# Four buffers of gathered expert rows instead of three

## The reference

```python
x = x + tanh(g_xattn) * attn(layernorm(x), ctx)   # attn: gelu(xn @ ctx.T) @ ctx, per batch
x = x + tanh(g_ffn) * moe(layernorm(x), gate_w, w1, w2, w3)

# moe: 8 experts, 256 hidden numbers each; every row goes to its two best experts
scores = softmax(xf @ gate_w); top_scores, top_idx = top_k(scores, 2)
xs = top_score * xf
y += (silu(xs @ w1[e]) * (xs @ w3[e])) @ w2[e]     # for both experts e of the row
```

## Time and profile before

| what | us |
|---|---|
| median of 3 runs | 688.33 |
| lowest and highest | 687.57, 690.29 |
| the profiled execution, its own time | 688.32 |
| its span (first to last instruction) | 686.6 |
| PE busy | 636.1 (93%) |
| POOL busy | 395.6 (58%) |
| ACT busy | 460.6 (67%) |
| DVE busy | 416.9 (61%) |
| mean granted TensorE clock, share of full | 0.991 |

### The profile page before, as it was taken

How to read it: one execution, slowest core, us unless ns; L and a number is a source line. 1 busy time by engine, 2 the same in 40 slices (tenths; PEclk the granted TensorE clock), 3 DMA queues, 4 the chain that set the end, 5 groups by cost and what they waited for, 6 DMA issues and landing times.

```text
span 686.6 us, 15832 instructions
## 1 busy us (share of the span) xinstructions
PE 636.1 (93%) x4638; PEld 442.9 (65%) x4639; DVE 416.9 (61%) x1287; ACT 460.6 (67%) x771; POOL 395.6 (58%) x459
## 2 busy tenths in 40 slices
PE   2789999999999999999998999999999999999990
PEld 1677788788887888878885555455554554555550
DVE  3368788898889888898886644543333333333330
ACT  5899999899998999999974444444443444434440
POOL 4332347765666656776566777875555555565551
PEclk9999999999999999999999999999999999999996
DMA  7455558646686567666424565766666656666653
GB/s 216 128 171 157 160 150 200 182 143 181 163 171 195 160 154 189 174 170 179 119 83 120 93 132 93 121 102 120 111 108 121 117 100 122 111 108 118 118 102 55
DMA packets 51380, 94.77 MB, mean 138 GB/s; under 512 B 17024, under 2 KB 25344, under 8 KB 51312
## 3 DMA queue, kind: packets, MB, share of 16 engines
q1 hardware_dynamic: 34096, 60.02, 32.9%
q0 software_dynamic: 16400, 33.89, 27.6%
q10 hardware_dynamic: 816, 0.02, 0.1%
HBM read 61.89 MB, written 32.01 MB: 137 GB/s over the span
## 4 chain that ended last, share of the span: by engine, by line
DMA 26%; PE 11%; issue 5%; DVE 3%; POOL 3%; ACT 1%; POOLq 1%; SPq 0%; DVEq 0%; ACTq 0%
DMA out_rows<-ctx_raw,meta 23%; PE bank L1368 5%; DMA ctx_raw<-xf_rows,meta 3%; PE bank L1377 3%; POOL out_rows L537 2%; PE bank L1323 1%; POOLq L533 1%; PE bank L1357 1%; ACT ctx_raw L766 1%; DMA meta<-route_table 0%; PE bank L1257 0%; PE bank L1222 0%; POOL ctx_raw L525 0%; DVE ctx_part L825 0%; DVE ctxT L1155 0%
## 5 line engine op out<-in xcount | busy, mean ns | idle before, releaser
L1368 PE MATMUL bank<-w,ctxT 128*128 x756 | 173.4, 379 | 0.9 <-issue 0.9
L537 POOL DMA_INDIRECT out_rows<-ctx_raw,meta x63 | 100.3, 1593 | 99.4 <-DMA out_rows<-ctx_raw,meta 87.8
L1222 PE MATMUL bank<-ctx_part,a_part 125*112 125x512 f16 x576 | 135.1, 380 | 0.8 <-DVE a_part L834 0.8
L1368 PEld LDWEIGHTS bank<-w,ctxT 128*128 128x128 f16 x756 | 74.0, 98 | 75.9 <-issue 1.0
L1210 PE MATMUL bank<-xnT,ctxT 128*125 128x224 f16 x1152 | 118.2, 262 | 0.3 <-ACT ctxT L629 0.3
L1210 PEld LDWEIGHTS bank<-xnT,ctxT 128*125 128x125 f16 x1152 | 112.4, 139 | 0.4 <-issue 0.4
L777 ACT ACTIVATE ctxT<-bank,cols 128x256 f32<-128x256 f32 x63 | 29.9, 474 | 115.4 <-issue 84.8
L1222 PEld LDWEIGHTS bank<-ctx_part,a_part 125*112 125x112 f16 x576 | 71.4, 130 | 39.6 <-DVE a_part L834 0.8
L629 ACT ACTIVATE ctxT<-bank 128x1000 f16<-128x1000 f16 x96 | 94.5, 1005 | 3.0 <-PE bank L1177 3.0
L1377 PE MATMUL bank<-w2s,ctxT 128*128 x378 | 91.9, 379 | 1.5 <-DVE ctxT L1137 1.5
L489 POOL DMA_INDIRECT route_table<-route,pos_i x64 | 72.8, 1138 | 19.2 <-issue 17.2
(11 more groups left out here) (155 smaller groups left out, 987.5 us busy)
## 6 DMA issues: line engine op xcount, KB each, us to landing
ctx_raw<-in_ctx SPq DMA_DIRECT2D x48, 448.0 KB
w_raw<-in_L_ffn_w SPq DMA_DIRECT2D x24, 512.0 KB, 6.3
x<-in_x SPq DMA_DIRECT2D x16, 448.0 KB, 6.5
out_rows<-x SPq DMA_DIRECT2D x16, 448.0 KB
xf_rows<-xf SPq DMA_DIRECT2D x16, 448.0 KB, 4.4
ctx_raw<-in_ctx SPq DMA_DIRECT2D x48, 52.0 KB
meta<-route_table SPq DMA_DIRECT2D x66, 1.0 KB, 2.0
ctx_raw<-xf_rows,meta POOLq DMA_INDIRECT x66, 4.2
```

The costliest lines, as they stand in the source:

```text
L537: g.indirect_dma_start(out=out, out_offset=bass.IndirectOffsetOnAxis(ap=meta[n][:, 0:1], axis=0), in_=y_sb[n % 2], in_offset=None, compute ...
L1222: ins = t_.matmul(O_ps[t][0:TT, :], a_part[ha][:, c, t * TT:(t + 1) * TT], ctx_part[u][hc][:, c, :], start=c == 0 and (ha, hc) == PARTS[0] ...
L1368: ins = t_.matmul(H_ps[u][:, :], rows, w, start=m == 0, stop=m == KD * len(PARTS) - 1)
```

## The change

```diff
-AHEAD = 3
+AHEAD = 4
...
-        bidx, landed_at, mapped, m_base = (xn[0:1, 0, lo:lo + n] for lo, n in ((4 * NBM, NBM), (5 * NBM, NBM + 2), (6 * NBM + 2, E + 1), (6 * NBM + E + 3, 1)))
+        bidx, landed_at, mapped, m_base = (xn[0:1, 0, lo:lo + n] for lo, n in ((4 * NBM, NBM), (5 * NBM, NBM // 2 * 2 + 2), (6 * NBM + 2, E + 1), (6 * NBM + E + 3, 1)))
```

## The result

| what | before | after |
|---|---|---|
| median, us | 688.46 (6 runs, 686.90 to 690.29) | 682.04 (6 runs, 681.07 to 683.91) |
| ratio to before, 95% interval | | 0.9914 (0.9899 to 0.9929) |
| the profiled execution, us | 688.32 | 682.06 |
| its span, us | 686.6 | 680.4 |
| mean granted TensorE clock | 0.991 | 0.992 |

The change makes the kernel 0.86% faster, 6.4 us. The forecast was 682.9. The time and the removed wait came as forecast; which engine sets the end afterwards did not.

The account below looks back on a forecast made before the run. POOL and PE delaying each other in a circle bound the kernel; afterwards POOL's scatter chain would set the end. Saving 193.5 - 188.2 = 5.3 us, 688.3 - 5.3 = 683.0, taken as 682.9; range 680.3 to 687.2.

Parts of the forecast that it names:

- The circle of POOL and PE: Second stage: late scatters delay gathers, gathers delay PE's transposes about 0.5 us per place, and late PE output delays scatters again.
- One block more is enough: Second stage: issuing each gather one block, 4.54 us, earlier removes PE's wait for gathers altogether.
- POOL's own chain: POOL's scatters of blocks 21 to 62: own cost 188.2 us against 193.51, setting the end and the 5.3 us gain.
- 22 ordinary steps: POOL, scatter to scatter within an expert: 4.36 us each, taken as only POOL's own work.
- The price of a new expert: POOL's step at an expert's first block, waiting for the scatter before to land: 5.64 us, nine times.
- PE's bare pace: PE's transposes, blocks 10 to 63: 4.54 us a block, 240.6 against 249.3 us, so at most 7.7 us to gain.
- PE sets the end: Rival for the second stage: POOL's steps shrink, scatters landing at 4.7 us, and all 7.7 us come; 680.6, chance 0.10.
- The output buffers cost nothing: ACT's output waiting for scatters to land, around block 48: 2.7 us wait, 1.3 us off the path, costed at nothing.
- this rival: Rival: ACT waiting for output buffers hands the scatters' lag back, 2.7 us passing into the chain; 685.7, chance 0.12.
- The head: Before the first scatter: POOL's extra gather of 1.0 to 1.3 us falls into idle time; cost 0, uncovered 1.3.
- Scatters land later: Rival: reads and adding writes meet differently on DMA engines, 0.7 us at each of 14 landing waits; 692.8, chance 0.06.
- The signs of being wrong: Profile after: PE still waiting for gathers, 4.8 us scatter steps remaining, last scatter directly following its output, or new-expert steps not 5.64.

Follow-up runs that it names:

- first experiment: Changed kernel with four gather buffers, but POOL's step b still gathering block b+3 as in the kernel before: 689.86 us, ratio 1.0021.
- light kernel with three output buffers: Changed kernel with 8 of 12 up matmuls per block (output less exact) and three output buffers instead of two: 657.25 us, ratio 0.9541.

## Why the prediction was right, and where not

- **The circle of POOL and PE.** Right. The places with a late gather had S steps of 4.7 to 5.3; after the change none of T's spacings names a gather behind block 1, and leaving the place in the list as it was (first experiment) brings all of it back.
- **One block more is enough.** Right; five ahead adds nothing.
- **That it takes a fourth buffer.** The prediction did not ask. It takes none: three with the same order do it.
- **POOL's own chain, 188.2 us from S(21) to S(62), sets the end.** Wrong, though the measured 189.3 is near it. The mis-sized term is the 22 ordinary steps at 4.36. Their own cost is 3.2 us (S(33) to S(35) in the light kernel with three output buffers). In the changed kernel they took 4.46 us in the mean all the same, since Y came only at PE's pace; that is why the sum came out near. The price of a new expert, 5.64, held: its nine steps took 5.49 to 5.72. The reason for the error is in the earlier trace rows: the 1.48 us idle before S(44) was taken for POOL's work at any time, while it is there only when Y comes after the gather has begun. The step S(24), 4.00, and S(43), 3.82, already showed that it can be shorter; the prediction gave that to the position behind a new expert instead of to Y's earliness. S(56), 3.18 behind S(55) in the same trace, is one of the 22 and was passed over.
- **PE's bare pace saves at most 7.7 us.** The right engine, with a saving that was 2.0 us too large: it saved 5.7. The turns of the loop cost 2.2 us in the changed kernel and not the 1.0 read from T(40) and T(52). T(28) has one as well; in the trace of before its lateness was put down to the gather alone. T(40) and T(52) showed 0.90 and 0.58 instead of 0.71 and 0.31; why these grew is not shown. The other 0.8 us are small delays, most of them before T(20) (T(16) comes 4.86 after T(15)), which the sum took as removable. The rival "PE sets the end" (680.6, chance 0.10) had the right engine, though POOL's steps shrank in another way than it named, to 3.2 us and not to 3.82; with 1.2 us more for the turns it would have given 681.8.
- **The output buffers cost nothing.** Right for the changed kernel, but for another reason. The lag of S over Y did not grow to 4.8 us: at S(46) it was 596.91 - 593.61 - 2.11 = 1.2, since POOL catches up by up to 1.4 us a step and not by 0.2. Where PE is made faster this rival costs time (41.4 us of ACT's waits, 11.3 us of the time), and with the loops written out ACT already waits (8.8 us).
- **The head.** Right: S(0) follows T(0) by 14.69 us instead of 14.63.
- **Scatters land later.** They did not: the median stayed 4.9 us, the longest went from 5.6 to 6.2.
- **The signs of being wrong.** S steps of 4.8 and more remained while T ran at 4.54: S(25) 5.42, S(55) 5.03, neither at a new expert. The prediction took such steps for the circle alone. The sign for a wrong bound, that S(62) follows Y(62) at once, could not appear, since S(62) waits for the landing of S(61) in both kernels. What did follow Y at once were the scatters before it: S(59) to S(61) start 1.4 us behind the end of their Y, both before and after.
- The estimate of 2.6 us for a gather, from the Trainium skill's page "DMA: Bandwidth & Descriptors", section on the anatomy of one DMA, does not fit the changed kernel's trace either: 4.2 us in the median, as before.

That the time came within 0.9 us of the forecast is therefore partly luck: two bounds, each off by some microseconds, lay close to each other.

## What to carry to other kernels

A buffer's depth and the place at which its load is issued are two things: before adding a buffer, look whether the load stands behind a slow wait in its issuer's list although its buffer has long been free; moving the issue may do all of it. An engine's step that looks rigid in a trace may contain a stretch that only appears when its input comes late; take its own cost from the shortest steps, and ask what was early there. And when a wait is removed, count the delays that stood hidden behind it, here at the turns of a loop.

## What the runs showed of the hardware

- A turn of the hardware loop costs PE 0.6 to 0.9 us in the trace of the changed kernel, at each of three places (0.69, 0.90, 0.58), with no releaser named; written out, all three places are at the bare 4.54. The size is not fixed: with three buffers and the new order, with five ahead, and with more work on POOL, single turns were 0.16 to 1.03 us late, 1.6 to 1.9 in all three.
- POOL's preparation of an indirect DMA varied little in the changed kernel: 1.56 to 1.65 us for a scatter, 0.95 to 1.32 for a gather (median 1.00). The 1.4 us between a gather and the next scatter of the same expert shrinks to 0.3 when the scatter's input was ready before the gather began, in all but a few places.
- At S(25) and S(55) POOL waited until the scatter before had landed (5.42 and 5.03 us after it) although neither begins an expert; S(55) did so in the kernel before too (4.94), and both do in the runs with three buffers (5.56, 5.11), with the loops written out (5.55, 5.28) and with more work on POOL (5.45, 5.06). No run was made on this, and its cause stays open.
